# Attention and mixture-of-experts layer on one core: first and last group re-ordered, two probability masks moved to ScalarE and GpSimd

## The chip, the cores and the metric

The kernel runs on one core of a Trainium2 chip. The metric is the device time of one execution in microseconds (us). Besides three timed runs there is one profiled execution, from which every row below comes. Times of rows are counted from the start of its span. The engines are TensorE (PE, matmuls; PEld is its weight load), VectorE (DVE), ScalarE (ACT), GpSimd (POOL) and SyncE (SP), which issues nearly all DMAs.

## The reference

Input are 4096 tokens (16 sequences of 256) of width 128, all in f32.

```
q, k, v = x Wq + bq, x Wk + bk, x Wv + bv        (16 heads of 8)
q, k    = exp(q), exp(k)
num, den = causal sums of q k v and of q k        (linear attention)
x1      = layernorm(x + (num / den) Wo + bo)
scores  = sigmoid(x1 gate_w)                      (32 experts in 4 groups)
w       = weights of the 8 best experts of the 2 best groups, scaled by 2.5
y       = sum over experts of w * down(silu(gate(x1)) * up(x1)) + shared expert
out     = layernorm(x1 + y)
```

## The kernel before, in words

Tokens go in 8 groups of 512. All 33 hidden layers of 64 or 128 units (32 experts and a shared one) are laid out as 17 **blocks** of 128 rows; block 0 is the shared expert. Every matmul of a block is done three times with fp32r halves (hi*hi, hi*lo, lo*hi), each 128x512.

A **slot** (n, g) is the unit of the order. In slot n of group g, `up(n, g)` (L352) computes the block's gate and up products on PE (six matmuls), ACT takes silu of the first (L656), DVE multiplies with the second (L955, "gated"), POOL multiplies with the expert weights in weight_wide (L1057, semaphore hidden_done), ACT copies the result to hidden_hi (L637), DVE or POOL forms hidden_lo (L781, L1097), and `down(n, g)` (L378, three matmuls) is issued LAG = 4 slots later. The buffers are a ring of 4: silu of slot n waits for hidden_lo of slot n - 4.

Beside the feed-forward part of group g, the same slots carry three others: "mid" for group m = g + 1 (attention's products, layernorm 1, gate, choice of experts), "front" for group f = g + 2 (projections, exponentials, masks, states) and "tail" for group g - 1 (layernorm 2, store). `schedule` (L221) calls each engine's own `slot` function in one written order, and each engine executes its own list strictly in that order; semaphores hold one engine for another. Before group 0 there are slots without feed-forward (g = -2, -1); there PE is given products whose result is not read (`keep_warm`, L393, counts in WARM, L30) where it would stand idle.

Where the change touches it:

- Start: SP loads attn_w, attn_cols, xT, constants, rows, then gate, up and down weights (L248 to L268). PE forms the bias product (L350), then the k and q projections (L551, L556); ACT takes their exponentials (L684, L687).
- Group 1's attention, in group 0's slots: scores of sequence 0 (L607), the sums den (L498), scores of sequence 1 (L508), `between_chunks` and `within_chunks`. DVE masks each score bank with tri into probs (`masked_probs`, L784): bank i counts probs_done up by one; i = 0 to 3 are sequence 0, 4 to 7 sequence 1. `between_chunks` (L410) waits for i = 4, since it writes that bank.
- First loads of the expert weights: `load_first` (L310) sends blocks 1, 2 and 3 to 4 apart (first_loaded), since POOL needs them at once.
- Choice of experts for group 7, in group 6's slots: x1 turned by PE at slot 9 (L539) and copied by ACT (L669, L672), gate product (L467) and exponential (L677) at slot 10, turned back at slot 11 (L448); DVE: expert_scores and group_tops at slot 10, masked_experts at 11, expert_weights at 12. PE turns the weights at slot 14 (L594), ACT copies (L726), SP writes them to DRAM (L294) and loads them spread over the partitions (L334): `load_wide(p, ...)` for blocks 4p + 1 to 4p + 4, 1 MB in two DMAs.
- Group 7 takes block 1 first and the shared block 0 last (`block_at`, L213), so that block 16 stands in slot 15.

## Time and profile before

| | |
|---|---|
| median of three runs | 458.29 us (457.49 to 458.95) |
| profiled execution, own time | 457.99 us |
| its span | 456.2 us |
| busy PE, DVE, POOL, ACT | 425.7, 345.7, 290.6, 275.8 us |
| granted TensorE clock, mean | 0.994 |

The time of an execution is 1.8 us more than its span. Between the first group and the last the program repeats itself, about every 52 us. In a row of the timeline the first number is the start, the second the time until the last of the xN instructions ended, and the square brackets say how long the engine stood idle before and who released it.

### The profile page before, as it was taken

Reading aid. Unit: us, or ns where it says so; the run is one execution under the profiler, and the core shown is the slowest. Engines: PE = TensorE matmul, PEld = TensorE weight load, DVE = VectorE, ACT = ScalarE, POOL = GpSimd, SP = SyncE. Lnnn points to the kernel's source line nnn. Section 1 sums busy time; section 2 is a strip of 40 time slices with the busy share of each in tenths; the row PEclk is TensorE's granted clock in tenths of the full one; section 3 lists DMA queues with packets and bytes.
Section 4 is the critical chain, followed back from the end, with each engine's and each line's share of the span. In section 5 each row is a group of like instructions: output and inputs, shape, how many; then the busy total and the mean of one; then the engine's idle time right before and its main releaser. Section 6 shows DMA issues by size and latency. Waiting matters only on the chain.

```text
span 456.2 us, 10923 instructions
## 1 busy us (share of the span) xinstructions
PE 425.7 (93%) x4004; PEld 327.3 (72%) x4004; DVE 345.7 (76%) x912; ACT 275.8 (60%) x536; POOL 290.6 (64%) x217
## 2 busy tenths in 40 slices
PE   5888999999999999999999999999999999798992
PEld 3656787768776887868777787868877787476771
DVE  2648777896979877896968967796968968767653
ACT  3746357763696448763696448863697347445642
POOL 2555368745797368754797377755687467666781
PEclk9999999999999999999999999999999999999997
DMA  7500664145454453245463453245452443348300
GB/s 238 210 1 7 174 129 88 34 94 132 96 124 91 102 117 96 49 94 118 93 138 84 100 128 85 57 99 116 93 139 51 104 102 86 61 100 183 94 24 23
DMA packets 28677, 45.10 MB, mean 99 GB/s; under 512 B 2000, under 2 KB 10320, under 8 KB 28240
## 3 DMA queue, kind: packets, MB, share of 16 engines
q1 hardware_dynamic: 28624, 44.40, 40.9%
q8 instruction: 32, 0.52, 0.5%
q14 instruction: 21, 0.17, 0.1%
HBM read 41.77 MB, written 2.62 MB: 97 GB/s over the span
## 4 chain that ended last, share of the span: by engine, by line
PE 31%; DVE 29%; issue 13%; POOL 11%; ACT 5%; DMA 2%; DVEq 1%; ACTq 0%; SPq 0%; POOLq 0%
PE bank L345 30%; DVE units L955 7%; POOL units L1057 6%; DVE stats L801 2%; DVE hidden_lo L781 2%; DVE top_of_group L842 2%; POOL rstd L1076 2%; DVE bank L835 2%; POOL xT_lo L1083 2%; DVE x L813 2%; DMA weight_wide<-weight_d 1%; ACT v_pair L718 1%; ACT hidden_hi L637 1%; DVE replaced L874 1%; DVE out_sb L967 1%
## 5 line engine op out<-in xcount | busy, mean ns | idle before, releaser
L1057 POOL TENSOR_TENSOR units<-units,weight_wide 128x512 f32<-128x512 f32 x128 | 177.4, 1391 | 115.6 <-DVE units L955 106.7
L656 ACT ACTIVATE units<-bank 128x512 f32<-128x512 f32 x136 | 80.7, 594 | 74.0 <-PE bank L345 73.8
L781 DVE TENSOR_TENSOR hidden_lo<-units,hidden_hi 128x512 fp32r<-128x512 f32 x112 | 99.7, 892 | 23.3 <-ACT hidden_hi L637 23.3
L637 ACT ACTIVATE hidden_hi<-units 128x512 fp32r<-128x512 f32 x136 | 86.0, 633 | 51.1 <-POOL units L1057 49.4
L955 DVE TENSOR_TENSOR units<-bank,units 128x512 f32<-128x512 f32 x136 | 93.1, 685 | 29.8 <-PE bank L345 22.7
L345 PE MATMUL bank<-x_hi,gate_hi 128*128 128x512 f32 x136 | 62.1, 456 | 5.1 <-DVE units L955 4.8
L345 PE MATMUL bank<-x_hi,up_hi 128*128 128x512 f32 x136 | 54.5, 401 | 2.9 <-ACT units L656 2.9
L345 PE MATMUL bank<-hidden_hi,down_hi 128*128 128x512 f32 x136 | 54.9, 404 | 2.5 <-DVE hidden_lo L781 1.3
L345 PE MATMUL bank<-x_lo,gate_hi 128*128 128x512 f32 x136 | 54.1, 397 | 0.0
L345 PE MATMUL bank<-x_hi,gate_lo 128*128 128x512 f32 x136 | 53.9, 396 | 0.0
L345 PE MATMUL bank<-x_hi,up_lo 128*128 128x512 f32 x136 | 53.9, 396 | 0.0
L345 PE MATMUL bank<-hidden_hi,down_lo 128*128 128x512 f32 x136 | 53.6, 394 | 0.0
L345 PE MATMUL bank<-hidden_lo,down_hi 128*128 128x512 f32 x136 | 53.6, 394 | 0.0
L345 PE MATMUL bank<-x_lo,up_hi 128*128 128x512 f32 x136 | 53.5, 393 | 0.0
L791 DVE TENSOR_TENSOR probs<-bank,const 128x512 f32<-128x512 f32 x64 | 40.5, 679 | 3.1 <-PE bank L345 3.1
L345 PEld LDWEIGHTS bank<-x_hi,gate_hi 128*128 128x128 f32 x136 | 25.5, 188 | 19.2 <-DVE units L955 7.5
L345 PEld LDWEIGHTS bank<-x_hi,up_hi 128*128 128x128 f32 x136 | 25.6, 188 | 12.5 <-ACT units L656 6.3
L345 PEld LDWEIGHTS bank<-hidden_hi,down_hi 128*128 128x128 f32 x136 | 25.5, 188 | 11.0 <-issue 4.0
L1097 POOL TENSOR_TENSOR hidden_lo<-units,hidden_hi 128x512 fp32r<-128x512 f32 x24 | 31.0, 1294 | 0.0
L345 PEld LDWEIGHTS bank<-x_hi,gate_lo 128*128 128x128 f32 x136 | 25.6, 188 | 6.0
L345 PEld LDWEIGHTS bank<-x_hi,up_lo 128*128 128x128 f32 x136 | 25.5, 188 | 6.0
L345 PEld LDWEIGHTS bank<-hidden_hi,down_lo 128*128 128x128 f32 x136 | 25.5, 188 | 5.8
(125 smaller groups left out, 689.2 us busy)
## 6 DMA issues: line engine op xcount, KB each, us to landing
weight_wide<-weight_d SPq DMA_DIRECT2D x62, 512.0 KB, 6.6
xT<-xT_in SPq DMA_DIRECT2D x8, 256.0 KB, 6.7
x_tok<-x_in SPq DMA_DIRECT2D x8, 256.0 KB, 7.0
out_dram<-out_sb SPq DMA_DIRECT2D x7, 256.0 KB, 2.3
weight_wide<-up_in SPq DMA_DIRECT2D x1, 1088.0 KB, 8.5
up_raw<-up_in SPq DMA_DIRECT2D x1, 1088.0 KB, 10.6
down_raw<-down_in SPq DMA_DIRECT2D x1, 1088.0 KB, 12.8
weight_d<-weightT SPq DMA_DIRECT2D x8, 64.0 KB, 1.6
```

The source lines that it names most:

```text
L345: return nc.tensor.matmul(out, lhsT, rhs, start=start, stop=stop, **k)
L637: nc.scalar.activation(hidden_hi[place(n, g)][:, :], units[place(n, g)][:, :], ACT.Copy).then_inc(hidden_hi_done, 1)
L656: nc.scalar.activation(units[place(n, g)][:, :], up_banks[2 * n % 3][:, :], ACT.Silu).then_inc(silu_done, 1)
L781: V.tensor_tensor(hidden_lo[place(n, g)][:, :], units[place(n, g)][:, :], hidden_hi[place(n, g)][:, :].bitcast(F32), ALU.subtract).then_in ...
L791: V.tensor_tensor(probs[:, b, q, :, :, :].rearrange("p c j s -> p (c j) s"), score_bank(m, i)[:, :].rearrange("p (c s) -> p c s", s=CHUNK) ...
L801: last = V.bn_stats(st[:, i, :], rows[:, i, :])
L813: last = V.tensor_scalar(dst[:, i, :], rows[:, i, :], mv[:, i, 0:1], rstd[:, i:i + 1], ALU.subtract, ALU.mult)
L835: linked(V.reciprocal(score, exp_neg), m, 2)
L842: last = V.max(top_of_group[:, k, :], by_group(choice[:, :])[:, k, :])
L955: V.tensor_tensor(units[place(n, g)][:, :], up_banks[(2 * n + 1) % 3][:, :], units[place(n, g)][:, :], ALU.mult).then_inc(gated_done, 1)
L1057: G.tensor_tensor(units[place(n, g)][:, :], units[place(n, g)][:, :], weight_wide[:, w % (2 * PIECE), :], ALU.mult).then_inc(hidden_done, 1)
L1097: G.tensor_tensor(hidden_lo[b][:, :], units[b][:, :], hidden_hi[b][:, :].bitcast(F32), ALU.subtract).then_inc(pool_lo_done, 1)
```

## The change

It does the following:

1. Start: ACT's queue issues the first xT load, SP no longer does; neg_half and a new zeroed tile `unread` are written by DVE before it waits; PE multiplies `unread` four times (128x256) before it waits for attn_w; the bias product moves behind the q projection, its addition (`rows_bias`) behind the running sums of k. The load of down_raw is issued later, after up_raw has landed and after group 1's rows.
2. Group 1's attention: the running sums of k (`k_totals(1)`) move from DVE's slot 14 to right behind layernorm 1 of group 0. Block 3's up products stand ahead of den, in place of three unread products (WARM den 3 to 0). Score banks 2 and 3 are copied by ACT into probs (probs_copied) and masked there by POOL (probs_masked); DVE waits for both before it masks bank 4. ACT's hidden_hi of blocks 1, 2, 3 are all in slot 4.
3. Choice of experts for group 7 alone (m = 7): x1 is turned at slot 8, the gate product and exponential follow at 9, turned back at 10; DVE's five steps lie in slots 10, 11, 12, 13, 14; PE turns the weights at slot 15. In group 7 the second load (p = 1) is issued right behind the first and no longer waits for POOL's first product.
4. In group 7, block 16 (slot 15) is multiplied with its weights by DVE, not by POOL.

Cut to its core:

```diff
-WARM = {"x1": 6, "x1T": 2, "up": 1, "weight": 4, "den": 3, "between": 2}
+WARM = {"x1": 6, "x1T": 2, "up": 1, "weight": 4, "den": 0, "between": 2}
...
-            if g == 0 and n in (1, 2, 3):
-                return ((), (0,), (1, 2))[n - 1]
+            if g == 0 and n in (1, 2, 3, 4):
+                return ((), (0,), (), (1, 2, 3))[n - 1]
...
+            return 9 if m < GROUPS - 1 else 8
...
+            return 14 if m < GROUPS - 1 else 15
...
-            steps(0, 0, 1, 2, mid=True)
-            steps(0, *range(3, SLOTS), ffn=True, mid=True, front=True)
+            steps(0, 3, ffn=True)
+            steps(0, 0, 1, 2, 3, mid=True)
+            steps(0, 3, front=True)
+            steps(0, *range(4, SLOTS), ffn=True, mid=True, front=True)
...
+                    if m == GROUPS - 1:
+                        load_wide(1, m, 1 - u)
...
+            pe.wait_ge(setup_chain, 2)
+            for _ in range(4):
+                mm(y_bank[:, 0:256], unread[:, 0:128], unread[:, 128:384])
             pe.wait_ge(w_attn_loaded, 32)
-            pe.wait_ge(setup_chain, 1)
-            mm(mid_banks[0][:, 0:DIM], bv_wide[:, :], woT).then_inc(bias_mm, 1)
...
+            nc.scalar.dma_start(xT[:, :], xT_d[:, 0:GROUP]).then_inc(xT_loaded, 16)
...
+                if front and f == 1 and n == 16:
+                    act.wait_ge(o_ready, 1)
+                    for q in (2, 3):
+                        act.wait_ge(scores_ready, SEQS * QUADS + q + 1)
+                        nc.scalar.activation(probs[:, 0, q, :, :, :].rearrange("p c j s -> p (c j s)"),
+                                             score_bank(1, q)[:, :], ACT.Copy).then_inc(probs_copied, 1)
...
+                if g == GROUPS - 1 and block_at(n, g) == ROUTED:
+                    dve.wait_ge(wide_loaded[PIECES - 1], loads_of(PIECES - 1, GROUPS))
+                    dve.wait_ge(gated_done, BLOCKS * g + n + 1)
+                    V.tensor_tensor(units[place(n, g)][:, :], units[place(n, g)][:, :],
+                                    weight_wide[:, 2 * PIECE - 1, :], ALU.mult).then_inc(last_hidden_done, 1)
...
+                    if m == 1 and n == 1:
+                        dve.wait_ge(probs_masked, 2)
+                        dve.wait_ge(scores_ready, SEQS * QUADS + QUADS + 1)
+                        dve.sem_inc(probs_done, 2)
...
+                if mid and n == (10 if m < GROUPS - 1 else 11):
                     group_tops(m)
-                if mid and n == 11:
+                if mid and n == (11 if m < GROUPS - 1 else 12):
                     masked_experts(m)
-                if mid and n == 12:
+                if mid and n == (12 if m < GROUPS - 1 else 13):
+                    chosen_experts(m)
+                if mid and n == (12 if m < GROUPS - 1 else 14):
                     expert_weights(m)
...
+                if front and f == 1 and n == 16:
+                    for q in (2, 3):
+                        pool.wait_ge(probs_copied, q - 1)
+                        own = probs[:, 0, q, :, :, :].rearrange("p c j s -> p (c j) s")
+                        G.tensor_tensor(own, own, tri.unsqueeze(1).to_broadcast([128, 2 * CHUNKS, CHUNK]), ALU.mult
+                                        ).then_inc(probs_masked, 1)
```

The order of the instructions at the three places of which the prediction speaks. First POOL in the prologue, from down_lo (the last of the prologue's weight splits) on, before (units is the product with expert weights):

```order
L1109 TENSOR_TENSOR down_lo<-down_raw,down_hi 128x2176
L1046 TENSOR_TENSOR k_sum<-k_sum,qT 128x512
L1057 TENSOR_TENSOR units<-units,weight_wide 128x512 x3
L1032 TENSOR_TENSOR x_bias<-x_tok,row_bias 128x512
L1057 TENSOR_TENSOR units<-units,weight_wide 128x512 x3
```

and in the change:

```order
L1168 TENSOR_TENSOR down_lo<-down_raw,down_hi 128x2176
L1099 TENSOR_TENSOR k_sum<-k_sum,qT 128x512
L1110 TENSOR_TENSOR units<-units,weight_wide 128x512 x2
L1147 TENSOR_TENSOR probs<-probs,const 128x512 x2
L1110 TENSOR_TENSOR units<-units,weight_wide 128x512
L1085 TENSOR_TENSOR x_bias<-x_tok,row_bias 128x512
```

The two masks stand behind the products of blocks 1 and 2.

DVE at the same place, from block 2's gated product on, before:

```order
L955 TENSOR_TENSOR units<-bank,units 128x512
L781 TENSOR_TENSOR hidden_lo<-units,hidden_hi 128x512
L791 TENSOR_TENSOR probs<-bank,const 128x512 x8
L962 RECIPROCAL inv_den<-den_cols 128x128
L955 TENSOR_TENSOR units<-bank,units 128x512
```

and in the change (the x3 are blocks 0, 1 and 2; the x4 wait for probs_masked):

```order
L995 TENSOR_TENSOR units<-bank,units 128x512 x3
L818 TENSOR_TENSOR hidden_lo<-units,hidden_hi 128x512
L828 TENSOR_TENSOR probs<-bank,const 128x512 x2
L995 TENSOR_TENSOR units<-bank,units 128x512
L828 TENSOR_TENSOR probs<-bank,const 128x512 x4
L1011 RECIPROCAL inv_den<-den_cols 128x128
```

Two of eight masks are gone from DVE, and block 3's gated product stands between the others.

DVE in group 6's slots, choice of experts for group 7, before, from slot 10's gated product on (exp_neg, score: bank):

```order
L955 TENSOR_TENSOR units<-bank,units 128x512
L834 TENSOR_SCALAR bank<-bank 128x128
L835 RECIPROCAL bank<-bank 128x128
L836 TENSOR_TENSOR choice<-bank,gate_bias 128x128
L842 MAX top_of_group<-choice 128x8 x16
L955 TENSOR_TENSOR units<-bank,units 128x512
...
L863 SCALAR_TENSOR_TENSOR masked<-bank,choice 128x128
L955 TENSOR_TENSOR units<-bank,units 128x512
L870 MAX top_vals<-masked 128x8 x4
L874 MATCH_REPLACE replaced<-top_vals,masked 128x32 x4
L878 SCALAR_TENSOR_TENSOR weight<-replaced,bank 128x128
```

and in the change:

```order
L995 TENSOR_TENSOR units<-bank,units 128x512
...
L873 TENSOR_TENSOR choice<-bank,gate_bias 128x128
L995 TENSOR_TENSOR units<-bank,units 128x512
L879 MAX top_of_group<-choice 128x8 x16
L995 TENSOR_TENSOR units<-bank,units 128x512
...
L900 SCALAR_TENSOR_TENSOR masked<-bank,choice 128x128
L995 TENSOR_TENSOR units<-bank,units 128x512
L907 MAX top_vals<-masked 128x8 x4
L911 MATCH_REPLACE replaced<-top_vals,masked 128x32 x4
L818 TENSOR_TENSOR hidden_lo<-units,hidden_hi 128x512
L995 TENSOR_TENSOR units<-bank,units 128x512
L918 SCALAR_TENSOR_TENSOR weight<-replaced,bank 128x128
```

Between the scores and the weights now stand four gated products (slots 11 to 14) and a hidden_lo, where two gated products stood.

## Rows read from the trace of the kernel before

**Rows 1.** The page, busy time by engine.

```profile
PE 425.7 (93%) x4004; PEld 327.3 (72%) x4004; DVE 345.7 (76%) x912; ACT 275.8 (60%) x536; POOL 290.6 (64%) x217
```

**Rows 2.** Timeline of the start, PE and ACT: start, us, engine, line, operation, [idle <-releaser].

```profile
5.38 3.75 PE L345 MATMUL bank<-xT,attn_w 128*128 128x512 f32 x4 [0.44 <-DMA xT<-xT_in]
9.17 0.69 ACT L687 ACTIVATE qT<-bank,attn_cols 128x512 f32<-128x512 f32 x1 [1.02 <-PE bank L345]
11.96 1.32 ACT L625 ACTIVATE q_heads<-qT,const 128x512 f32<-128x512 f32 x2
```

**Rows 3.** Timeline of PE further on in the prologue.

```profile
25.04 1.88 PE L345 MATMUL bank<-xT,attn_w 128*128 128x512 f32 x4
26.75 2.75 PE L345 MATMUL bank<-attn_w 128*128 128x256 f32 x12
```

**Rows 4.** Windows, end of the program: stretch, length, busy PE PEld DVE ACT POOL, PEclk, DMA.

```profile
450.40:456.20 5.80, 0.00 (x0) 0.00 (x0) 1.67 (x10) 0.88 (x2) 1.21 (x2) 0.50 0.15 45
```

**Rows 5.** Timeline of PE, group 1's attention.

```profile
46.43 1.56 PE L345 MATMUL bank<-attn_w 128*128 128x256 f32 x6
...
49.37 1.21 PE L345 MATMUL bank<-q_heads,kT 32*64 32x128 f32 x64 [0.77 <-DVE probs L791]
...
51.47 0.88 PE L345 MATMUL bank<-qT,kv_blocks 128*128 128x192 f32 x6
...
53.31 0.50 PE L345 MATMUL bank<-x_hi,gate_hi 128*128 128x512 f32 x1
...
56.66 0.50 PE L345 MATMUL bank<-x_hi,gate_hi 128*128 128x512 f32 x1
```

**Rows 6.** Timeline of DVE, ACT and POOL at the same place.

```profile
50.56 2.48 DVE L791 TENSOR_TENSOR probs<-bank,const 128x512 f32<-128x512 f32 x4 [1.25 <-PE bank L345]
45.31 2.55 ACT L718 ACTIVATE v_pair<-v_tok 64x128 f32<-64x128 f32 x8
50.26 2.51 POOL L1057 TENSOR_TENSOR units<-units,weight_wide 128x512 f32<-128x512 f32 x2 [3.88 <-DMA weight_wide<-weight_d]
```

**Rows 7.** Timeline of PE, DVE and ACT in group 6, slots 8 to 14.

```profile
380.57 1.37 DVE L813 TENSOR_SCALAR x<-bank,mean_var,rstd 128x128 f32<-128x128 f32 x4 [0.30 <-POOL rstd L1076]
380.43 0.40 PE L345 MATMUL bank<-x_hi,gate_hi 128*128 128x512 f32 x1
382.54 0.60 PE L539 MATMUL bank<-const,x 128*128 128x128 f32 x4
383.62 0.58 ACT L669 ACTIVATE x1T<-bank 128x512 f32<-128x512 f32 x1
388.37 0.30 DVE L834 TENSOR_SCALAR bank<-bank 128x128 f32<-128x128 f32 x1 [1.08 <-PE bank L448]
389.46 0.60 ACT L656 ACTIVATE units<-bank 128x512 f32<-128x512 f32 x1
398.28 0.29 DVE L883 TENSOR_TENSOR weight<-weight,bank 128x128 f32<-128x128 f32 x1
398.63 0.61 PE L594 MATMUL bank<-const,weight 128*32 128x128 f32 x4 [0.88 <-DVE weight L883]
```

**Rows 8.** Windows, group 6's slots 12 to 14; columns as in rows 4.

```profile
388.00:399.00 11.00, 7.79 (x33) 5.07 (x31) 8.28 (x46) 5.27 (x9) 7.41 (x6) 1.00 0.29 59
```

**Rows 9.** Timeline of POOL and PE at the head of group 7.

```profile
409.16 2.53 POOL L1057 TENSOR_TENSOR units<-units,weight_wide 128x512 f32<-128x512 f32 x2 [2.83 <-DMA weight_wide<-weight_d]
411.65 0.51 PE L345 MATMUL bank<-x_hi,up_hi 128*128 128x512 f32 x1 [0.45 <-ACT units L656]
415.88 0.47 PE L345 MATMUL bank<-hidden_hi,down_hi 128*128 128x512 f32 x1 [1.15 <-ACT yT L647]
```

**Rows 10.** Timeline of the end, POOL and PE.

```profile
443.18 1.67 POOL L1057 TENSOR_TENSOR units<-units,weight_wide 128x512 f32<-128x512 f32 x1 [1.23 <-DVE units L955]
444.58 0.39 PE L345 MATMUL bank<-hidden_hi,down_lo 128*128 128x512 f32 x1
446.29 0.50 PE L345 MATMUL bank<-hidden_hi,down_hi 128*128 128x512 f32 x1 [1.32 <-DVE hidden_lo L781]
```

More of the change, by code:

```diff
@@ L78, in attention_moe_kernel @@
         neg_half = sb("neg_half", [128, TILES])
+        unread = sb("unread", [128, 384])
         xT = sb("xT", [128, GROUP])
@@ L252, in slot @@
                 m, f = g + 1, g + 2
-                if front and n == 5:
+                if front and f > 0 and n == 5:
                     at = f * GROUP
@@ L260, in slot @@
                     load_rows(f)
+                    if f == 1:
+                        sp.wait_ge(up_loaded, 16)
+                        sp.sem_inc(apart, 1)
+                        sp.dma_start(down_raw, down_d).then_inc(down_loaded, 16)
                 if g == -2 and n == 5:
@@ L328, in load_wide @@
                     sp.sem_inc(apart, 1)
-                sp.wait_ge(hidden_done, reached(ROUTED * g + (1 if p == 1 else PIECE * (p - 1))))
+                sp.wait_ge(hidden_done, reached(ROUTED * g + (1 if p == 1 and g < GROUPS - 1 else PIECE * (p - 1))))
                 sp.sem_inc(apart, 1)
@@ L460, in slot @@
                     down(BLOCKS - LAG + n, g - 1)
-                if mid and n == 10:
+                if mid and n == turned_at(m) + 1:
                     if m == 0:
@@ L471, in slot @@
                     down(n - LAG, g)
-                if mid and not front and n == (10 if m == 0 else 11):
+                if mid and not front and n == 10:
                     turn_exponentials(m)
@@ L532, in slot @@
                     last.then_inc(proj_ready, 1)
-                if mid and n == 9:
+                if mid and n == turned_at(m):
                     if m == 0:
@@ L558, in slot @@
                         turn_exponentials(m)
+                if g == -2 and n == 11:
+                    pe.wait_ge(setup_chain, 3)
+                    mm(mid_banks[0][:, 0:DIM], bv_wide[:, :], woT).then_inc(bias_mm, 1)
                 if front and n == 11:
@@ L632, in high_part @@
                     act.wait_ge(gated_done, reached(BLOCKS * g + n + 1))
+                elif g == GROUPS - 1 and block_at(n, g) == ROUTED:
+                    act.wait_ge(last_hidden_done, 1)
                 else:
@@ L664, in slot @@
                     last.then_inc(inv_copied, 1)
-                if mid and n == 9:
+                if mid and n == turned_at(m):
                     act.wait_ge(x1_turned, reached(m + 1))
@@ L999, in slot @@
                 if front and f == 0 and n == 14:
+                    rows_bias()
                     dve.wait_ge(q_exp, 1)
```

46 lines of the change are left out of this document (27 added, 19 removed).

## Prediction

> **What bounds the kernel now.** I read the page first: PE is busy for 93% of the span [rows 1], so in the middle groups nothing but PE work or PE idleness can change the time, and the change does not touch them. What it touches are the two ends, so I read the timelines of all engines there, one engine after the other, and asked of each stretch who is waited for last. At the start PE, ACT and DVE hand one chain to each other from the first projection to the first x1; no engine is full. In group 1's attention PE waits for DVE's masks, and POOL stands idle until the first expert weights have landed [rows 5, 6]. In group 6 from slot 10 on DVE is the engine waited for, since the choice of experts stands between gated products [rows 7]. At the head of group 7 PE waits for what follows from the load of the expert weights [rows 9]; its last such wait there ends at 415.88. The end is one chain through block 16 [rows 10].
>
> I sum against the profiled execution (457.99 us, its span plus 1.8); the median of the runs is 0.3 us more. About 0.3% (1.4 us) can be told from no change.
>
> **Part 1, the start.** The k and q projections take 3.75 us for four passes [rows 2]; the same four take 1.88 later [rows 3], so at 5.38 the array runs at 1.2 GHz, the lower of its two levels. Twelve unread passes of 256 columns take 2.75 us at the upper level [rows 3], 0.23 each, so the eight new ones take 0.46 each at the lower, 3.7 us. I estimate that DVE has `unread` written by 1.3 us, so they fill PE until about 5.1. xT, issued a microsecond earlier, should be there by then; it was at 5.38 before. So the projections begin only 0.3 us earlier, but the array has been at work for almost 4 us. Before, all four passes stayed slow, 3.75 us and more behind the first; I take 5 us from 1.3, so the rise at 6.3. Of the 3.75 us 1.2 are done by then, the rest takes 1.3: q's projection ends near 7.6 instead of 9.13. Its exponential was at 9.17 right behind it [rows 2], and the following items of ACT (v, k, the masked queries at 11.96) are in a row behind that; k's exponential gains less. I take **-1.3 us**; bounds are -0.3 (only the earlier start) and -2.2 (all four passes at the upper level). The bias product and rows_bias cost nothing where they now stand, before q is there. down_raw lands later, but ACT needs it last of all; its cover is some 2 us, and if it went, ACT's down_hi would delay the next projections.
>
> The Trainium skill, "TensorE: Matmul & The Clock Gate", section "What's actually happening", says that the moment of the rise depends on where the matmuls fall in a free-running count and so moves from run to run. One trace cannot show this; by it the sum of this part is anything between the two bounds, not one value.
>
> **Part 2, group 1's attention.** All times here are in the frame of the old trace; the 1.3 us come off later. k's running sums filled a wait of DVE and fill another now: nothing. Block 3's up products (six passes) stand where 1.56 us of unread ones stood [rows 5], and leave the place at 53.31. Den runs at about 47.8. Behind it everything turns on two in-order lists:
>
> ACT does four v_pair (half of 2.55 us from 45.31 [rows 6]), the two copies (0.6 each, as silu, which also reads a bank, at 389.46 [rows 7]), four v_pair, silu of block 3, den_cols: until 49.9. Scores of sequence 1 wait for that: 49.9 to 51.1, 0.5 later than before [rows 5].
>
> POOL's masks stand behind the products of blocks 1 and 2. Those wait for the first load and run from 50.26 to 52.8 [rows 6]. Nothing in the change brings this load closer to the scores, since both hang on the same chain. Two masks of 1.26 each, as these products, end at **55.3**. DVE may not touch bank 4 before; it did at 50.56. `between_chunks` waits for bank 4: it starts at 56.0 instead of 51.47 [rows 5]. PE then has between and within for both sequences left in a row: twice 1.84 (the first from 51.47 to 53.31), so block 4's up products begin at 59.7 instead of 56.66: +3.0, block 3 being done in both. The copies to hidden_hi of blocks 1 to 3 now stand behind inv_denT, so down of block 1 and the second half of block 6's up wait for them: another 0.7. From there on PE is full, so nothing is given back: **+3.7 us**. Bounds: +1.5 (the copies and DVE's masks hidden in part, half of the wait found again) and +4.3 (masks at 1.67 each, as the product at 443.18 [rows 10]).
>
> **The clock.** Behind the scores four unread passes keep PE for 0.9 more, then it stands idle from 52.0 to 56.0, and it has only 2.1 us of work between 48.3 and 56.0. At the end of the program the granted clock is 0.50 from 450.4 on [rows 4], the lower level, 2.5 us behind the last product of a block (down(16) follows down(15) of 446.29 [rows 10], 0.7 us each, and ends at 447.9) and with less than a microsecond of PE's work between. These 5.8 us are all that is missing from the mean of 0.994, so it falls nowhere else after the start. I take it that it falls in the new gap, and that the climb lasts as at the start, 3.75 us or a little more: half of it is lost. **+2.0 us**; bounds 0 and +2.9.
>
> **Part 3, choice of experts for group 7.** x1 is ready at 381.94 [rows 7]; slot 8's place on PE ends at 380.43 [rows 7], so PE stands for 1.5 us, and the turned x1 is with ACT at 382.7 instead of 383.62, 0.9 earlier. ACT's row from x1T to the silu after the exponential, 383.62 to 390.06 [rows 7], has 0.5 more in it now (out_sb of tail inside, a wait out): silu of slot **10** ends at 389.6. DVE's list has gated(10) ahead of the scores, so these start at 390.2 and not at 388.37 [rows 7]: +1.8. Between them and the weights DVE has three more items of 0.6 (two gated, one hidden_lo): +1.8. The weights are ready at **402.1** instead of 398.57 [rows 7]. From there to POOL's first product it was 10.6 us (transposes, copy, store, 1 MB of load), which the change doesn't shorten: 412.7 instead of 409.16. Behind that stand hidden_hi(0), silu(2), the second half of up(3) (411.65), and down(0) at 415.88 [rows 9]; all go 3.5 later. PE gets back part of its idle 3.2 us between 388 and 399 [rows 8], but spends it at 400 and at 412. After 415.88 PE has next to no wait until 444.97, so **+3.5 us** stay; the second load, now right behind the first, lands about when it did, and POOL, later itself, no longer waits for it: -0.3. Bounds: +1.5 (if the chain through ACT's tables is 2 us shorter than I read it) and +5 (the clock also falls in PE's wait of 3.3 us at 412).
>
> **Part 4, block 16.** POOL's product takes 1.67 [rows 10], DVE's about 0.7 (as its masks, 2.48 for four [rows 6]). But DVE has then hidden_lo(14) and gated(16) ahead of hidden_lo(15). down(15) at 445.7 instead of 446.29 [rows 10]: **-0.6**, bounds 0 and -1.3 (until PE is out of other work, at 444.97 [rows 10]).
>
> Sum: -1.3 + 3.7 + 2.0 + 3.5 - 0.3 - 0.6 = **+7.0**, so 465.0 for such an execution, 465.3 as a median.
>
> **Rivals.**
> A, the same without the fall of the clock: +5.0, 463.3. For it: PE is dense until 48.3, and the one fall in the trace is no law. Chance 0.22.
> B, the clock falls at 412 too, where PE waits 3.3 us: +1.5 more, 466.8. The Trainium skill, "TensorE: Matmul & The Clock Gate", section "HAM oscillation — how this bites in real kernels", describes this: each wait between bursts is paid a second time as slow matmuls. By that rule B is the likelier; the old trace shows one fall, at the end. Against it: PE has 1.15 us to spare before down(0) anyway [rows 9]. Chance 0.15.
> C, faster: the list through ACT is not what holds silu(10), and DVE finds its work ready, so that spreading the choice over five slots gives PE its 3.2 us between 388 and 399 [rows 8] back, with the weights no later than 398.6. It decides where silu of slot 10 ends: before about 386 the weights are on time. That is -3.2 in place of +3.5; and POOL's masks are through when the scores of sequence 1 are (51.1), which leaves -1.0 in place of +5.7. With start and end -6.1, 452; with one of the two places so and the other half so, 456. For it: PE's idleness at both places is real and would be removed. Against it: both lists as printed. Chance 0.19, and 0.07 that gains and losses meet within 0.3%.
> Left for the forecast: 0.37.
>
> **How the numbers follow.** 465.3 is the likeliest case. Slower: 0.37 + 0.22 + 0.15 = 0.74. The range reaches up to 469 (B with the upper bounds of masks and clock) and down to 457.5, through A with its lower bounds into the case of no change; it leaves out C.
>
> **What would show it.** The masks on POOL start behind 50, DVE's row of the four masks has an idle of 4 to 5 us released by POOL, and `between_chunks` starts 4 to 5 us behind the end of the scores. PEclk under 1.00 between 53 and 61. In group 6: PE waits 1.5 us for x1 at slot 8; weights some 12 us behind the start of the scores instead of 10.2; POOL's wait for weight_wide at the head of group 7 over 5 us. I am wrong if the masks run before the products of blocks 1 and 2, or if the last group's first product comes no later, counted from group 6's start.

## The result and the profile after

The changed kernel takes 465.69 us (median of four executions, 465.44 to 466.20), the kernel before on the same chip 458.15 (457.49 to 458.95): a ratio of 1.0166, 95% interval 1.0151 to 1.0181. It is slower by 7.5 us, and the forecast of 465.3 holds. The profiled execution took 466.20 us, 8.2 more than the one of before (457.99); the stages below are summed against these two.

The page of the change, the line of busy times and the row of TensorE's granted clock in 40 slices:

```profile
PE 430.3 (93%) x4006; PEld 331.3 (71%) x4006; DVE 343.9 (74%) x912; ACT 276.5 (60%) x538; POOL 289.5 (62%) x218
PEclk9999899999999999999999999999999999988998
```

PE has two passes more than in [rows 1] (eight unread ones at the start, six fewer ahead of den), yet it is busy for 4.6 us longer. 2.2 us of this are the exchange of unread passes (3.78 us for the eight, 1.56 for the six [rows 5]); for the rest, the same work ran slower in places. A slice is 11.6 us. The clock row has dents in the fifth slice (46 to 58 us) and in the two from 406 to 430, beside the end of the program; between them it is whole.

To place the difference I cut each execution at four events that every kernel here has: PE turns x1 of group 0 (end of the start), DVE writes x1 of group 7 (in group 6's slots; the expectations call it x1 of group 6), POOL begins the first product of group 7, and PE begins to turn the last yT. From the last one to the end of the time it is 9.5 us in every kernel.

| stage, us | before | change | difference | forecast |
|---|---|---|---|---|
| start, to x1 of group 0 | 30.21 | 28.57 | -1.64 | -1.3 |
| to x1 of group 7 | 350.36 | 356.12 | +5.76 | +3.7 + 2.0 |
| to the first product of group 7 | 28.59 | 33.02 | +4.43 | +3.5 - 0.3 |
| to the last turning | 39.35 | 39.00 | -0.35 | -0.6 |

They sum to +8.20. The first row is flattered by the kernel before. In its profiled execution PE stood still once in the prologue, with no releaser that the trace shows:

```profile
20.11 0.52 PE L345 MATMUL bank<-probs,v_pair 128*32 128x64 f32 x18 [1.34 <-issue]
```

From PE's product with k_sum (15.40) to the turning of x1 it took 14.81 us there; in all twelve kernels with the new start it took 13.87 to 14.00. DVE, which forms attnT behind it, waits 2.02 us for PE there and 1.22 in the change. So 0.9 of the 1.64 us go with this pause, and 0.7 are the change. Only one trace of the kernel before exists, so whether its other executions pause too is not shown.

**Group 1's attention.** Timeline of PE in the change (columns as in [rows 2]; the xN of long groups are instructions):

```profile
48.39 1.20 PE L363 MATMUL bank<-q_heads,kT 32*64 32x128 f32 x64 [1.85 <-ACT den_cols L766]
49.52 1.13 PE L363 MATMUL bank<-attn_w 128*128 128x256 f32 x4
54.30 1.02 PE L363 MATMUL bank<-qT,kv_blocks 128*128 128x192 f32 x6 [3.65 <-DVE probs L828]
55.25 1.94 PE L363 MATMUL bank<-probs,v_pair 128*32 128x64 f32 x64
57.12 1.62 PE L363 MATMUL bank<-qT,kv_blocks 128*128 128x192 f32 x6
58.67 1.10 PE L363 MATMUL bank<-probs,v_pair 128*32 128x64 f32 x64
59.70 0.50 PE L363 MATMUL bank<-x_hi,gate_hi 128*128 128x512 f32 x1
...
64.87 0.50 PE L363 MATMUL bank<-hidden_hi,down_hi 128*128 128x512 f32 x1 [0.57 <-DVE hidden_lo L818]
65.69 0.39 PE L363 MATMUL bank<-x_hi,gate_hi 128*128 128x512 f32 x1
```

DVE and POOL at the same place:

```profile
53.47 2.48 DVE L828 TENSOR_TENSOR probs<-bank,const 128x512 f32<-128x512 f32 x4 [4.59 <-POOL probs L1147]
...
48.36 2.50 POOL L1110 TENSOR_TENSOR units<-units,weight_wide 128x512 f32<-128x512 f32 x2 [8.25 <-DMA weight_wide<-weight_d]
50.81 2.49 POOL L1147 TENSOR_TENSOR probs<-probs,const 128x512 f32<-128x512 f32 x2
```

Read it backwards: PE idles 3.65 us for DVE's mask of bank 4, DVE 4.59 us for POOL's masks, and POOL has stood for 8.25 us waiting for a load, with the masks queued behind it. The masks' data, ACT's copies, were there from 46.2 on (L739, two copies of 0.6 from 45.08). Against [rows 5], counted from the turning of group 0's x1, block 4's up products come 4.68 us later and block 6's 5.54. The window in which the four steps behind the wait run (start:end, length, busy PE PEld DVE ACT POOL, PEclk, DMA share, GB/s):

```profile
55.00:60.00 5.00, 5.00 (x138) 4.55 (x138) 1.81 (x3) 0.00 (x0) 0.75 (x1) 0.66 0.44 96
```

**The choice of experts for group 7.** DVE, PE and POOL in the change, and two windows (columns as above):

```profile
384.69 1.37 DVE L850 TENSOR_SCALAR x<-bank,mean_var,rstd 128x128 f32<-128x128 f32 x4 [0.30 <-POOL rstd L1129]
394.39 0.29 DVE L871 TENSOR_SCALAR bank<-bank 128x128 f32<-128x128 f32 x1
406.17 0.29 DVE L923 TENSOR_TENSOR weight<-weight,bank 128x128 f32<-128x128 f32 x1
...
406.51 0.96 PE L618 MATMUL bank<-const,weight 128*32 128x128 f32 x4 [2.08 <-DVE weight L923]
420.17 0.72 PE L363 MATMUL bank<-x_hi,up_hi 128*128 128x512 f32 x1 [2.37 <-ACT units L683]
...
417.71 2.48 POOL L1110 TENSOR_TENSOR units<-units,weight_wide 128x512 f32<-128x512 f32 x2 [5.18 <-DMA weight_wide<-weight_d]
```

```profile
405.00:410.00 5.00, 3.48 (x11) 2.77 (x12) 3.06 (x7) 2.23 (x4) 2.36 (x2) 0.66 0.05 13
420.00:425.00 5.00, 4.83 (x14) 3.83 (x15) 3.77 (x6) 3.12 (x7) 3.10 (x3) 0.66 0.23 45
```

From x1 to the scores it is 9.70 us (before 7.80), to the last weight 21.48 (before 17.71), and from the weights' turning to POOL's product 11.20 (before 10.53) [rows 7, 9]. The last wait of POOL in the change is 5.18 us. The clock is at its lower level right behind both of PE's waits.

### The profile page after: what moved, and what is told of

It is laid out like the page before. It is cut to its first block, busy times and chain, and to the rows that moved or that the text cites. A ratio compares the mean times of both kernels' runs of the same rounds, so it can differ in the third digit from the quotient of the medians.

```text
span 464.4 us, 10932 instructions
## 1 busy us (share of the span) xinstructions
PE 430.3 (93%) x4006; PEld 331.3 (71%) x4006; DVE 343.9 (74%) x912; ACT 276.5 (60%) x538; POOL 289.5 (62%) x218
## 4 chain that ended last, share of the span: by engine, by line
PE 31%; DVE 28%; issue 14%; POOL 11%; ACT 6%; DMA 2%; DVEq 1%; ACTq 0%; SPq 0%; POOLq 0%
PE bank L363 30%; DVE units L995 7%; POOL units L1110 6%; DVE hidden_lo L818 2%; DVE stats L838 2%; DVE top_of_group L879 2%; POOL rstd L1129 2%; DVE bank L872 2%; POOL xT_lo L1136 2%; ACT hidden_hi L664 2%; DMA weight_wide<-weight_d 2%; DVE x L850 1%; ACT v_pair L751 1%; DVE replaced L911 1%; ACT units L683 1%
## 5 line engine op out<-in xcount | busy, mean ns | idle before, releaser
L1110 POOL TENSOR_TENSOR units<-units,weight_wide 128x512 f32<-128x512 f32 x127 | 174.6, 1379 | 127.7 <-DVE units L995 114.1
L818 DVE TENSOR_TENSOR hidden_lo<-units,hidden_hi 128x512 fp32r<-128x512 f32 x112 | 96.8, 866 | 24.6 <-ACT hidden_hi L664 24.4
L828 DVE TENSOR_TENSOR probs<-bank,const 128x512 f32<-128x512 f32 x62 | 39.3, 679 | 6.2 <-POOL probs L1147 4.6
L363 PEld LDWEIGHTS bank<-x_hi,up_hi 128*128 128x128 f32 x136 | 25.7, 189 | 14.6 <-ACT units L683 8.3
L363 PEld LDWEIGHTS bank<-x_lo,up_hi 128*128 128x128 f32 x136 | 25.8, 190 | 5.7
```

The source lines that it names most:

```text
L363: return nc.tensor.matmul(out, lhsT, rhs, start=start, stop=stop, **k)
L818: V.tensor_tensor(hidden_lo[place(n, g)][:, :], units[place(n, g)][:, :], hidden_hi[place(n, g)][:, :].bitcast(F32), ALU.subtract).then_in ...
L828: V.tensor_tensor(probs[:, b, q, :, :, :].rearrange("p c j s -> p (c j) s"), score_bank(m, i)[:, :].rearrange("p (c s) -> p c s", s=CHUNK) ...
L1110: G.tensor_tensor(units[place(n, g)][:, :], units[place(n, g)][:, :], weight_wide[:, w % (2 * PIECE), :], ALU.mult).then_inc(hidden_done, 1)
```

## The experiments

Every kernel was timed beside the kernel before on the same chip; ratios are to it. The stages of the profiled executions, as above (own time last):

| kernel | start | to x1 of 7 | to first product | to last turning | own |
|---|---|---|---|---|---|
| before | 30.21 | 350.36 | 28.59 | 39.35 | 457.99 |
| change | 28.57 | 356.12 | 33.02 | 39.00 | 466.20 |
| e1 masks by DVE | 27.76 | 352.73 | 32.61 | 38.88 | 461.48 |
| e2 choice as before | 27.54 | 356.13 | 28.92 | 38.91 | 460.98 |
| e3 second gap filled | 27.25 | 357.33 | 33.77 | 38.91 | 466.74 |
| e4 POOL's masks first | 28.16 | 353.41 | 32.46 | 39.02 | 462.55 |
| e5 start alone | 27.81 | 349.79 | 28.68 | 39.39 | 455.15 |
| e6 spread alone | 26.98 | 357.17 | 30.55 | 39.00 | 463.20 |
| e7 early turn alone | 27.19 | 355.89 | 30.61 | 38.91 | 462.10 |
| e8 combined | 27.09 | 347.97 | 28.62 | 38.96 | 452.12 |
| e9 both gaps filled | 27.54 | 356.21 | 33.77 | 39.77 | 466.81 |
| e10 four masks ahead | 28.09 | 349.02 | 32.73 | 39.04 | 458.35 |
| e11 combined, early load | 27.20 | 347.97 | 28.75 | 38.92 | 452.32 |

**e1, masks by DVE.** No copies by ACT, no masks by POOL:

```diff
-                if mid and n < 3 and not (m == 1 and n == 0):
-                    if m == 1 and n == 1:
-                        dve.wait_ge(probs_masked, 2)
...
+                if mid and n < 3:
```

> The change with one part taken back: DVE masks score banks 2 and 3 again, ACT copies nothing and POOL masks nothing; block 3's up products stay ahead of den. Theory (POOL's masks stand behind its products of blocks 1 and 2, and hold DVE, then PE, whose clock then falls): between_chunks starts at about 50.5 and not at 54.3, no fall of the clock at 55, down(1) about 5 us earlier; time 460.5 to 461.5, that is 4 to 5 us under the changed kernel's 465.7. Rival (not the masks but hidden_hi of blocks 1 to 3 behind inv_denT, or POOL's later start, holds PE): the stall is less, but up(6) stays behind 64 and the time stays over 463.5.

461.51 us, ratio 1.0067 (1.0050 to 1.0084), the upper edge of what was expected. The stage falls by 3.4 us, from +5.76 to +2.37. But PE is not free of waits:

```profile
48.22 1.62 PE L362 MATMUL bank<-q_heads,kT 32*64 32x128 f32 x64 [2.46 <-DVE probs L819]
49.77 2.07 PE L362 MATMUL bank<-attn_w 128*128 128x256 f32 x4
51.64 1.20 PE L362 MATMUL bank<-qT,kv_blocks 128*128 128x192 f32 x6
...
55.74 0.50 PE L362 MATMUL bank<-x_hi,gate_hi 128*128 128x512 f32 x1
```

The clock fell here too, only earlier: scores take 1.62 us instead of 1.20, the four unread passes 2.07 instead of 1.13. So the expectation that the clock would not fall was wrong, and 2.4 us of this stage are not POOL's masks. What PE waited for was DVE's second pair of masks, behind block 3's gated product (e10 tests this).

**e2, choice as before.** The second load stays early.

```diff
-            return 9 if m < GROUPS - 1 else 8
+            return 9
...
-            return 14 if m < GROUPS - 1 else 15
+            return 14
...
-                if mid and n == (10 if m < GROUPS - 1 else 11):
+                if mid and n == 10:
                     group_tops(m)
```

(likewise masked_experts at 11, the last two steps at 12, and turning back at 11).

> The change with the choice of experts for group 7 in its old slots (x1 turned at slot 9, DVE's steps at 10, 10, 11, 12, 12, weights turned by PE at 14); the second load stays right behind the first. Theory (what stands between scores and weights delays the load, and all behind it): from x1 of group 6 to the last product's transposes 4 to 5 us less, time 460.7 to 461.7. Rival (PE got its idle time of group 6 back, and the load's duration or the two falls of the clock at 407 and 420 come from elsewhere): the time stays within 1 us of 465.7. If the early second load slows the first, the load of group 7 stays longer than the 7.4 us of before, and some 0.3 us remain.

461.06 us, ratio 1.0070 (1.0055 to 1.0085), inside the first forecast. The third stage is back from 33.02 to 28.92, and the first load takes 7.76 us from its issue to POOL's product, 0.35 more than before (401.75 to 409.16 there): in this pair the early second load is a small loss.

**e3, the second gap filled.**

```diff
-WARM = {"x1": 6, "x1T": 2, "up": 1, "weight": 4, "den": 0, "between": 2}
+WARM = {"x1": 6, "x1T": 2, "up": 1, "weight": 4, "den": 0, "between": 10}
```

> The change with ten unread products instead of two each time ahead of between_chunks: 16 more of 0.23 us, 3.7 us, in PE's idle 3.65 us. Theory (the wait there is paid twice, the second time by products at the lower level of the clock): the granted clock stays 1.00 from 53 to 60, between and within take 3.7 us instead of 5.4, time 1.5 to 2 us under 465.7, so 463.7 to 464.2. Rival (the matmuls in 55 to 58.5 are slow for another reason, or their cost is hidden again by block 4): 465.7 within 0.4 us, or more if the unread products end too late.

467.16 us, ratio 1.0208 (1.0183 to 1.0232): 1.5 us above the change, where 1.5 to 2 us less were expected. It did not test what it was made for. PE in e3, and its window:

```profile
47.07 1.20 PE L363 MATMUL bank<-q_heads,kT 32*64 32x128 f32 x64 [1.85 <-ACT den_cols L766]
48.19 6.27 PE L363 MATMUL bank<-attn_w 128*128 128x256 f32 x20
54.30 0.88 PE L363 MATMUL bank<-qT,kv_blocks 128*128 128x192 f32 x6
```

```profile
45.00:50.00 5.00, 3.15 (x77) 2.50 (x70) 0.69 (x1) 1.86 (x6) 2.76 (x3) 0.86 0.54 160
```

Up to 48.19 this is the change's own code with the change's own wait of 1.85 us, and the clock fell during the unread passes, ahead of the gap that I had filled. In the change it had held until 55. The same code at the same wait gave a fall in one execution and none in the other. At the lower level the twenty unread passes took 6.27 us and held PE: between_chunks starts 27.05 us behind the turning of group 0's x1, against 25.73 in the change.

**e4, POOL's masks first.** The same lines, ahead of POOL's products of blocks 1 and 2:

```diff
-                if front and f == 1 and n == 16:
+                if g == 0 and ffn and n == 1:
                     for q in (2, 3):
                         pool.wait_ge(probs_copied, q - 1)
```

> The change with POOL's two masks ahead of its products of blocks 1 and 2, and not behind them: they start at about 46, where POOL waits for the first load. Theory (the in-order place is the cost, not the use of POOL): DVE's wait for probs_masked is gone, between_chunks starts at about 50.5, clock stays up; time 460 to 461.5, as or a little below the kernel with DVE's masks. Rival (the handoff over ACT and POOL itself is dear: copies, two more semaphores, POOL's masks slowed beside DVE's): between_chunks starts behind 52, time over 463.

459.70 us, ratio 1.0041 (1.0020 to 1.0062), 6.0 us under the change in the medians and a little under what was expected, by an exchange of two places in one list. POOL:

```profile
45.36 2.50 POOL L1107 TENSOR_TENSOR probs<-probs,const 128x512 f32<-128x512 f32 x2 [5.68 <-ACT probs L739]
47.82 2.49 POOL L1116 TENSOR_TENSOR units<-units,weight_wide 128x512 f32<-128x512 f32 x2
```

The masks run where POOL used to wait. between_chunks starts 23.5 us behind the turning of group 0's x1, not 25.7. So the handoff over ACT and POOL is cheap; its place was most of the cost. It is not free: PE waits 1.84 us for den_cols behind ACT's copies, v_pair and silu, where it waits 0.73 in e10, and e10's median is 0.6 us lower. One point was expected wrongly: the clock fell all the same in the profiled execution, at the scores (2.00 us for them). The profiled execution is one of the two slowest of ten (462.55; the others from 459.31), and it has a pause of PE of 0.89 us at 59.11 for which the trace shows no releaser; without it the stage is 3.6 us shorter than in the change.

**e5, start alone.** Part 1 of the change in the kernel before, in its core:

```diff
+            pe.wait_ge(setup_chain, 2)
+            for _ in range(4):
+                mm(y_bank[:, 0:256], unread[:, 0:128], unread[:, 128:384])
             pe.wait_ge(w_attn_loaded, 32)
```

> The kernel before with the change's part 1 alone (start, bias product behind, down_raw later). In the five traces with this start, x1 of group 0 was turned by PE at 27.25 to 28.57 against 30.21, and the moment at which the array had risen differed with it. Theory (the unread products bring the rise forward, by an amount that varies from execution to execution): time 1.6 to 3.0 us under the kernel before, middle 2.3, so about 455.8, and the projections take between 1.9 and 3.1 us. Rival (what is gained at the start is lost again by a later stage that waits for a load or for POOL, and the group 1 stage does not move with it): 457 or more; then the first expert weights land no earlier than in the kernel before.

455.15 us, ratio 0.9939 (0.9916 to 0.9961), 2.5 us faster in the medians, as expected. Nothing later gives it back. The run takes part 1 as a whole; what its single edits are worth is not tested.

**e6, spread alone, and e7, early turn alone.** Each makes one half of e2's edit. e6:

```diff
-            return 9 if m < GROUPS - 1 else 8
+            return 9
```

and e7, with all of DVE's steps in their old slots:

```diff
-            return 14 if m < GROUPS - 1 else 15
+            return 14
```

> The change with x1 of group 7 turned at slot 9 again (gate product, exponential and turning back one slot later too), but DVE's steps still in slots 10 to 14 and the weights turned at 15. The change as a whole costs 3.8 us here between x1 and the weights, and the kernel with both taken back was at 461.1. Theory (the gated products and the hidden_lo that stand between the steps cost the most of it): the scores start 7.8 us behind x1 as in the kernel before, the weights some 2 us later than there, time 462.5 to 463.5. Rival (the later scores are the whole cost, DVE catches up): time within 0.5 us of 461.1. Second rival (turning early was a gain inside a loss): 465 or more.

> The change with x1 of group 7 turned at slot 8, but DVE's steps in slots 10, 10, 11, 12, 12 again and the weights turned at 14. Theory (silu and gated product of slot 10 now stand ahead of the scores, behind PE's wait at slot 8): the scores still start 9.7 us behind x1 and not 7.8, the weights about 2 us later than in the kernel before, time 462.5 to 463.5; with the run that only spreads the steps the two parts add up to the 4.6 us. Rival (early turning is harmless when DVE's steps follow at once): within 0.5 us of 461.1.

463.07 us, ratio 1.0125 (1.0091 to 1.0158), and 462.84 us, ratio 1.0107 (1.0081 to 1.0133), both inside the first forecast. DVE's x1, scores and last weights in e6, then in e7:

```profile
384.15 1.36 DVE L850 TENSOR_SCALAR x<-bank,mean_var,rstd 128x128 f32<-128x128 f32 x4 [0.30 <-POOL rstd L1129]
391.92 0.30 DVE L871 TENSOR_SCALAR bank<-bank 128x128 f32<-128x128 f32 x1 [1.06 <-PE bank L467]
403.70 0.29 DVE L923 TENSOR_TENSOR weight<-weight,bank 128x128 f32<-128x128 f32 x1
```

```profile
383.08 1.37 DVE L850 TENSOR_SCALAR x<-bank,mean_var,rstd 128x128 f32<-128x128 f32 x4 [0.30 <-POOL rstd L1129]
392.79 0.29 DVE L871 TENSOR_SCALAR bank<-bank 128x128 f32<-128x128 f32 x1
402.68 0.29 DVE L923 TENSOR_TENSOR weight<-weight,bank 128x128 f32<-128x128 f32 x1
```

x1 to scores 7.77 and 9.71 us, x1 to weights 19.55 and 19.60, against 17.71 before: +1.84 and +1.89, together 3.73, and the change has +3.77. The two halves add up. In e7 the reason stands on ACT:

```profile
389.37 0.28 ACT L704 ACTIVATE exp_negT<-bank 128x128 f32<-128x128 f32 x1
...
390.19 1.28 ACT L683 ACT_TABLE_LOAD   x1
391.48 0.60 ACT L683 ACTIVATE units<-bank 128x512 f32<-128x512 f32 x1
```

ACT loads a table ahead of the exponential and another ahead of the next silu, 1.28 us each (ACT_TABLE_LOAD). One slot earlier, both loads lie ahead of silu of slot 10, whose gated product stands ahead of the scores on DVE.

e6 also shows that the clock's price in group 1 is not one number. Up to there it is the change's code, as in e2 and e7. But its clock was at the lower level from 52 to 59, where the change's was from 55 to 58.5, and its four steps from between_chunks to block 4's up products took 6.73 us (52.62 to 59.35); in the change, e2 and e7 they took 5.40. Its second stage is 1.05 us longer than the change's.

**e8, combined.** The start and block 16 of the change, up(3) ahead of den, choice and loads for group 7 as before, all masks on DVE, and two orders of my own:

```diff
                 if front and n == 16:
                     masked_probs(f, 0)
+                    if f == 1:
+                        masked_probs(f, 1)
...
+                if ffn and g == 0 and n == 4:
+                    for b in (1, 2, 3):
+                        high_part(b, g)
                 if ffn:
                     act.wait_ge(g_ready, reached(BLOCKS * g + n + 1))
```

(the same three in `low_part` on DVE, ahead of slot 4's gated product).

> The start and the block 16 of the change, up(3) ahead of den, all masks by DVE with the four of sequence 0 in a row ahead of block 3's gated product, hidden_hi and hidden_lo of blocks 1 to 3 ahead of silu and gated product of block 4, choice of experts and loads for group 7 as in the kernel before. Theory (up(3) in place of the unread products is a gain of 1.5 us if nothing on DVE or ACT is put in front of the scores; the start gives 2.3, the end 0.5): scores of sequence 1 some 18.7 us behind the turning of group 0's x1 instead of 20.5 in the kernel with DVE's masks, no wait of down(1), time 453 to 455. Rival (PE stays idle about 2 us ahead of the scores of sequence 1 for lack of work and its clock falls there whatever DVE does): 455.5 to 457.

452.18 us, ratio 0.9879 (0.9855 to 0.9903): 5.4 us faster than the kernel before, and 0.8 under the range expected. PE:

```profile
45.81 1.20 PE L360 MATMUL bank<-q_heads,kT 32*64 32x128 f32 x64 [0.74 <-DVE probs L820]
46.93 1.13 PE L360 MATMUL bank<-attn_w 128*128 128x256 f32 x4
47.90 0.88 PE L360 MATMUL bank<-qT,kv_blocks 128*128 128x192 f32 x6
...
51.69 0.50 PE L360 MATMUL bank<-x_hi,gate_hi 128*128 128x512 f32 x1
```

Scores start 18.72 us behind the turning of group 0's x1, the clock stays up, and down(1) does not wait. The same four steps from between_chunks to block 4's up products take 3.79 us here and 5.40 in the change: that is the clock's price there, **1.6 us** (2.9 in e6).

**e9, both gaps filled.** e3, and ahead of the scores of sequence 1:

```diff
+                        if m == 1:
+                            keep_warm(4)
                         pe.wait_ge(probs_done, SEQS * QUADS * m + (QUADS if m > 1 else 2))
```

> The change with both of PE's idle times around the scores of sequence 1 filled: four unread products ahead of them (8 passes, 1.85 us) and ten instead of two ahead of between_chunks. With only the second filled, the clock had fallen earlier, from about 48 on, and the twenty products took 6.27 us. Theory (PE's idleness makes the clock fall, at one of the two waits or the other): granted clock 1.00 from 45 to 60, between_chunks starts where DVE's mask allows it, 25.1 us behind the turning of group 0's x1 at the most (it was 25.7), the four stages behind it take 4.1 us and not 5.4; time about 1.5 us under the 465.7 of the change, 463.5 to 464.7. Rival (the clock falls here whatever PE does, or its cost is absorbed by waits further on): 465.7 within 0.5 us.

467.41 us, ratio 1.0200 (1.0154 to 1.0246); 463.5 to 464.7 was expected. Windows and PE of its profiled execution:

```profile
45.00:50.00 5.00, 5.00 (x88) 3.89 (x88) 0.69 (x1) 2.14 (x7) 2.72 (x3) 1.00 0.59 166
50.00:55.00 5.00, 4.86 (x84) 4.11 (x83) 2.60 (x5) 0.00 (x0) 4.70 (x4) 1.00 0.98 215
55.00:60.00 5.00, 3.72 (x92) 3.09 (x82) 0.74 (x1) 0.33 (x1) 0.00 (x0) 1.00 0.21 53
```

```profile
56.07 0.98 PE L363 MATMUL bank<-probs,v_pair 128*32 128x64 f32 x53
58.32 0.41 PE L363 MATMUL bank<-probs,v_pair 128*32 128x64 f32 x11 [1.28 <-issue]
```

The first half of the theory is borne out: with both gaps filled the clock is 1.00 from 45 to 60. The second is not: the time did not fall. In the profiled execution a pause of PE of 1.28 us, released by nothing that the trace shows, ate the gain on the spot, and the head of group 7 cost more than in the change: the first load took 8.47 us (7.74 there), and the clock was at its lower level from 418 to 425, around PE's wait of 4.06 us that ends at 420, with the last stage 0.8 us longer. The four executions spread from 464.99 (mean clock 0.995) to 470.39 (0.980). So the price of the clock rests on the steps' durations, not on a faster kernel.

**e10, four masks ahead.** e1 with the first of e8's two orders alone:

```diff
+                    if f == 1:
+                        masked_probs(f, 1)
```

> The kernel with DVE's masks (461.5) with the four masks of sequence 0 in a row, ahead of block 3's gated product and not two ahead and two behind; hidden_hi of blocks 1 to 3 stay behind inv_denT. Theory (the gated product waits for silu of block 3 behind eight v_pair copies on ACT, and two masks wait behind it): the scores of sequence 1 start 18.7 us behind the turning of group 0's x1 instead of 20.5, PE's clock does not fall there, and PE gets 1.8 us by the one and about 1.2 by the other: 458 to 459. Left of the group-1 stage is then the wait of down(1) for hidden_hi, about 1 us. Rival (the order of the masks costs nothing, and the combined kernel's gain came from hidden_hi placed ahead of silu of block 4): within 0.5 us of 461.5.

459.12 us, ratio 1.0021 (1.0010 to 1.0032), 2.4 us under e1 and at the upper edge of what was expected. The scores start at 46.80, 18.71 us behind the turning, with a wait of 0.73, and the clock holds there:

```profile
46.80 1.20 PE L362 MATMUL bank<-q_heads,kT 32*64 32x128 f32 x64 [0.73 <-DVE probs L819]
47.93 1.13 PE L362 MATMUL bank<-attn_w 128*128 128x256 f32 x4
```

The stage goes from 352.73 to 349.02, and e8's early hidden_hi takes it on to 347.97.

**e11, combined with the early second load.**

```diff
+                    if m == GROUPS - 1:
+                        load_wide(1, m, 1 - u)
```

> The combined kernel (452.2) with the change's early second load for group 7: issued right behind the first, no longer behind POOL's first product. Theory from the traces with it (from the issue of the first load to POOL's first product 7.54 to 8.85 us with both loads in flight against 7.41 in the kernel before and 7.44 in the combined one): the two loads share the queue and the first lands later, 7.6 to 7.8 us behind its issue; POOL's later wait of 2.2 us for the second load goes, but PE is not held by it; time 452.3 to 453.0. Rival (the prediction's term: POOL's later wait is on PE's path, 0.3 us are gained): 451.9, and the first load takes 7.44.

452.64 us, ratio 0.9883 (0.9861 to 0.9904); e8 had 0.9879. POOL's later wait for the second load (2.19 us at 412.52 in e8) has become one of 1.35 us for DVE, and PE's waits behind the head of the group are 0.61, 1.15 and 0.51 against 0.51, 1.17 and 0.54. The first load took 7.55 us against 7.44. No gain, and a loss of 0.1 in the profiled stage.

## Why the prediction was right

**Part 1** (-1.3, bounds -0.3 and -2.2): -1.64 in the profiled change, of which 0.9 us go with the old trace's pause at 20.11. So -0.7 came by the forecast way, and that the row comes out near -1.3 is luck. The steps, here of the change:

```profile
1.35 3.78 PE L363 MATMUL bank<-unread 128*128 128x256 f32 x8 [1.35 <-DVE unread L802]
5.52 2.84 PE L363 MATMUL bank<-xT,attn_w 128*128 128x512 f32 x4 [0.39 <-DMA attn_cols<-attn_cols_in]
8.39 0.69 ACT L714 ACTIVATE qT<-bank,attn_cols 128x512 f32<-128x512 f32 x1
```

The unread passes last to 5.1 as reckoned; here xT's earlier issue was of no use, since attn_cols came last; q's exponential is at 8.39 (before 9.17). The projections did not begin 0.3 us earlier but 0.14 later than before, 5.52 for 5.38. And the single moment of the rise failed. The granted clock reads 1.00 from the start to 10 us in both traces, so this rise is not in it, and the level can only be read from the durations. By these (an estimate: 0.47 us for an unread pass and 0.94 for a pass of the projections at the lower level, half at the upper) the rise lay at 7.4 us in the change, and between 4.3 (e11) and 7.4 in the twelve kernels with this start, where 6.3 was forecast. They reached x1 of group 0 between 26.98 and 28.57, mean 27.60, the profiled change last of all. Against the one old trace that is 1.6 to 3.2 us, mean 2.6; without the pause it is 0.7 to 2.3, mean 1.7 (e5 gained 2.5 in the medians; whether the kernel before pauses in its other executions too is open). So the bounds hold but for 0.1 us, which the eight passes of v can account for: they also became faster, 1.43 us where the kernel before took 1.75 at 8.92, and the bound counted only the projections. The Trainium skill, "TensorE: Matmul & The Clock Gate", section "What's actually happening", had said that the moment moves from run to run; the twelve traces agree, and its sentence in the prediction was the better forecast of this term.

**Part 2** (+3.7) and **the clock** (+2.0): together 5.7, measured 5.76. Every named step is there: POOL's masks at 50.81 behind the products, DVE idle for 4.59 us, released by POOL, between_chunks 4.7 us behind the end of the scores, up products of block 4 at +3.1 without the clock (forecast 3.0), the wait for hidden_hi another 0.9 (0.7), and the clock 1.6 (2.0). e4 shows the main cause: the place in POOL's list. The clock's 1.6 lies inside the bounds of 0 and 2.9, and e6 paid the 2.9. (The upper bound of the masks, 4.3, is too low by its own terms: 3.7 and 0.4 more for each of two masks are 4.5.) What the text did not see is the second in-order list: with POOL out of the way (e1), DVE's own masks behind block 3's gated product keep the scores back by 1.8 us (20.46 behind the turning in e1, 18.71 in e10), and PE's wait there lets the clock fall at another place.

**Part 3** (+3.5): +4.43 with the load. The two causes and their sizes, +1.8 and +1.8, are measured at +1.89 and +1.84. I had rounded their sum down to 3.5, and mis-sized what follows: PE turned the weights in 0.96 us instead of 0.61, since the clock fell right behind its wait of 2.08 us, and the load took 7.74 instead of 7.41. The term that failed in sign is the early second load, **-0.3**: it is +0.1 to +0.35 (e11, e2), since POOL's later wait was not on PE's path. The first load took 7.54 to 7.76 us in the eight kernels where the second followed at once (e3 and e9 left out), and 7.41 to 7.51 in the three where it did not; that the loads slow each other is the likely reason, and not shown. I had taken from POOL's wait what only PE's could give.

**Part 4** (-0.6): -0.35 in the change, -0.39 in e8 against the old trace. PE's last wait of 1.32 us [rows 10] became 0.28 and 0.24:

```profile
453.20 0.50 PE L363 MATMUL bank<-hidden_hi,down_hi 128*128 128x512 f32 x1 [0.28 <-DVE hidden_lo L818]
...
454.40 0.50 PE L363 MATMUL bank<-hidden_hi,down_hi 128*128 128x512 f32 x1 [0.24 <-DVE hidden_lo L818]
```

**The rivals.** A is refuted by the window 55 to 60, where the granted clock of the change is 0.66. B's mechanism did come true, twice: the clock fell behind PE's wait for the weights, which I had not named, and behind the wait that I had at 412 (here 2.37 us, ending at 420.17). Its price was some 0.4 us and not 1.5: 0.35 at the weights' turning, and a last stage only 0.1 us longer than e2's, which has no fall there. PE had to wait for group 7's hidden layers anyway: e2's wait of 1.17 us ahead of down(0) is not there in the change. The Trainium skill, "TensorE: Matmul & The Clock Gate", section "HAM oscillation — how this bites in real kernels", agrees with this trace on slow matmuls behind a wait; it prices a fall at half of the slow time, over 1 us for each of the two (an estimate by that section), and here they cost 0.35 and 0.1. C is out: spreading the steps gave PE no time back. Where it waits 0.74, 0.52 and 0.88 us between the scores and the weights in the kernel before, it waits once in e6, for 2.06 us.

So 7.0 against 8.2 in the profiled pair and 7.5 in the medians is no sum of large errors that cancel. The largest is part 3 with the load, 4.4 for 3.2; the next is part 1, -0.7 for -1.3, which the pause in the old trace covers. How close the median comes, 465.69 for 465.3, is in part luck: the range was 11.5 us wide, and executions of one kernel differ by 1 us and more.

## What to carry to other kernels

Before handing work to an engine that looks idle, read what its next instruction waits for: an instruction behind a wait for a load is as late as the load, and everyone who waits for it too; e4's exchange of two places was worth 6 us. An edit that spreads a chain over more slots must be judged by what is in the way between its links, above all on the path to a load, and not by the idle time of an engine that isn't waited for. Useful work in place of unread products gains only if the work behind it is ready: the same move of up(3) stands in a stage that is 2.4 us longer than before in e1, and 2.4 us shorter in e8. A baseline needs a second trace as well: a pause in one execution of it looked like a gain of 0.9 us.

## What the runs showed that I had not expected

- The clock fell beside waits of only 1.8 to 2.5 us (e1, e3, e4, and in e10 at two waits of 2.08 and 2.11 at the head of group 7), and with the same code on PE it fell at the scores in e4, right behind them in e3, and 6 us later in the change. The length of the wait does not decide it: PE waited 2.08 us for group 7's weights in the change, e3 and e10, and the clock fell; it waited 2.06 or 2.07 us at the same place in e1, e4, e6 and e9, and the clock held.
- Executions spread from 459.31 to 462.55 in e4 and from 464.99 to 470.39 in e9, but only from 452.07 to 452.99 in e8, in whose profiled execution the clock fell nowhere before the end. That the falls make the spread is not shown: the change has them too, and its four executions lie within 0.8 us.
- PE paused for 0.9 to 1.3 us without a releaser in the kernel before (at 20.11), e3 (at 113.74), e4 and e9, in kernels whose program there is the same as in others that did not pause. In the windows of all four the DMA view lists packets of an instruction queue, but so it does for the kernel before from 54 to 61, where PE did not pause. The cause stays open.
- The first load of group 7's weights took 8.85 and 8.47 us in e3 and e9, and 7.4 to 7.8 in all others. This too is open; in that stage the two filled kernels are 0.75 us slower than the change.
